# Splitting the context rows of a two-layer cross-attention kernel on ScalarE and VectorE instead of GpSimd, and the order in which two query groups are opened

## The chip, the cores and the metric

The kernel runs on one core of a Trainium2 chip. The metric is device time in microseconds (us), the median of several executions. A core has a matrix engine (TensorE, PE in the profile), a vector engine (VectorE, DVE), an activation engine (ScalarE, ACT), a general engine (GpSimd, POOL) and a queue engine that starts transfers (SyncE, SP). Each runs its own list of instructions in the order in which it was written; they meet at semaphores. PE writes to PSUM banks; ACT, DVE and POOL work on SBUF, and the first two also read PSUM.

## The reference

Two layers work on 2048 tokens of 256 features and on 1601 context rows of 256 features. Each layer is a cross attention followed by a mixture-of-experts network. The change lies in the cross attention of the second layer, where tokens attend to context and context to tokens:

```python
def _L1_xattn_ref(char_emb, subword_emb, ...):      # tokens, context
    ...
    scores = jnp.einsum('bqh,bkh->bqk', Q_char, K_sub) * scale
    char2sub = jnp.einsum('bqk,bkh->bqh', jax.nn.softmax(scores, axis=-1), V_sub)
    ...
    scores2 = jnp.einsum('bqh,bkh->bqk', Q_sub, K_char) * scale
    sub2char = jnp.einsum('bqk,bkh->bqh', jax.nn.softmax(scores2, axis=-1), V_char)
    L_char = char_emb.shape[1]
    if sub2char.shape[1] != L_char:
        sub2char = _interp_linear(sub2char, L_char)
    gate_in = jnp.concatenate([char2sub, sub2char], axis=-1)
    gate = jax.nn.sigmoid(jnp.einsum('blh,oh->blo', gate_in, Wg) + bg)
    return gate * char2sub + (1 - gate) * sub2char
```

`sub2char` has one row for each of the 1601 context rows; `_interp_linear` stretches it to 2048 rows, each a weighted mean of two neighbouring ones.

## The kernel before

**Precision.** TensorE multiplies numbers of a shortened float format. So each operand x is split in two: x_hi is x copied to that format, x_lo is x - x_hi. A product is then three matmuls: hi·hi, lo·hi, hi·lo (`mm3`, lines 43 to 45). Nearly every tile in the trace has the suffix `_hi` or `_lo` for that reason, and "a split" is a copy (often on ACT) and a subtraction (often on DVE).

**Groups, blocks, steps.** `cross_phase` does both attentions of the second layer. The queries stand in 14 groups. Groups 0 to 5 are the context rows (the "context half"): 13 row tiles of 128, two per group and three in group 5. Groups 6 to 13 are the 16 token tiles, two per group (a "token pair"). The keys of a group are cut in blocks, mostly two key tiles wide; all groups together have 112 blocks. Group 5 is blocks 40 to 55, group 6 blocks 56 to 62, group 7 blocks 63 to 69, group 8 blocks 70 to 76. The main part is a loop over steps n = 0 to 100, written out once for each engine; all its instructions have fixed places. For a block, in order of what depends on what:

- PE `score` (lines 43 to 45, output `wide`), ACT `evacuate` (line 2414) to a place in SBUF (tiles `Fx`, `sraw` or `X`), DVE `maximum` (line 2825 for the first block of a group, 2828 for the others; tile `rows`) and, at the last block of a group, a fold of the two halves (line 2832).
- Once per group: PE `max_turn` (line 2115, a transpose of the maxima), DVE `tops` (line 2838), ACT `spread_max` (line 2424), PE `spread_turn` (line 2122). After that the group's maximum lies on a PSUM bank, and the group can be opened.
- DVE `subtract` (line 2849), ACT `exponent` (line 2429), ACT `high` (line 2436, tile `pt`), DVE `low` (line 2854, tile `pt`), and PE `weighted` (lines 2140 to 2142), the product with the values. Step n holds `weighted(n)`; the others run ahead.
- After a group's last block DVE's `finish` (lines 2865 and 2879) divides by the sum, which frees PE's bank for the next group's first block. For a context tile the result is a row tile of `X`.

**What runs ahead by how much** is set by tables: `behind[n]` names the blocks whose scores stand in step n; `sub_end`, `exp_end` and `high_end` say up to which block the subtractions, the exponentials, and the high and low halves have come after step n. A group's subtractions start at step `open_from(g)`: 61 for group 7 and 68 for group 8. There `sub_end` jumps by four blocks, and `exp_end` follows a step later:

```python
sub_end = [reached(n, 5) for n in range(-1, NBLK)]
exp_end = [sub_end[0]] + sub_end[0:NBLK]
high_end = [min(reached(n, 2), e) for n, e in zip(range(-1, NBLK), exp_end)]
```

**Context rows.** The 13 finished row tiles in `X` are split into `CT_hi` and `CT_lo`, so that PE can interpolate them (`interpolate`, lines 2165 and 2166): a matmul with a "tent", a 128x128 matrix of interpolation weights. The first interpolation stands in step 61. The split is done in four pieces, `ROW_CHUNKS`: tiles 0-1, 2-5, 6-9 and 10-12. ACT copies the first two pieces to `CT_hi` (line 2562, steps 56 and 57); POOL copies the other two (line 2703) and subtracts all four (line 2707). All of it waits for the last block of the context half (`weighted_done` at `NSB` = 56). POOL makes the tents as well (`tents_of`: TENSOR_SCALAR in lines 2682 to 2689 and 2696, TENSOR_TENSOR in line 2690), four of them by the time of the first mixing; in its queue stand the tent of tile 0, the four row pieces, and the tents of tiles 1 to 3. The tents lie in the spare ends of `V_hi` and `V_lo`.

**Other work in these steps.** During group 5 PE also makes the keys and values of the token half (`later_unit`), whose high halves ACT copies (line 2392 for values) and whose low halves DVE subtracts (line 2811). At steps 47, 48, 49 and 57 one weight is split (`LATE`: lines 2591 and 3071).

## Time and profile before

| what | us |
|---|---|
| median of 3 runs | 978.98 |
| lowest and highest | 978.89, 980.35 |
| the profiled execution | 977.88 |
| its span, first to last instruction | 976.1 |
| PE busy in the span | 929.8 |
| DVE busy | 736.2 |
| ACT busy | 583.0 |
| POOL busy | 359.0 |

The span is what the profile shows of one execution; the few microseconds around it belong to starting and ending the program. PE's mean granted clock was 0.991 of full speed. A duration of a row is that of one execution of one instruction, or of several merged ones where it says x2 or more. Instructions on an engine overlap a little at their ends, so that a row of 0.68 us can be followed by the next start after 0.60 us.

### The profile page before, as it was taken

The page shows a single profiled execution, that of the slowest core. Times are in us where ns is not written, and L with a number is a line of the kernel's source. Part 1 is how long each engine was busy: PE and PEld are TensorE (multiplying, and loading weights), DVE is VectorE, ACT ScalarE, POOL GpSimd, SP SyncE. Part 2 cuts the span into 40 slices and gives each one's busy share as a digit, 9 for nine tenths or more (in the row PEclk, how much of TensorE's full clock was granted, in tenths as well). Part 3 has the DMA queues.
Part 4 walks back from the last instruction along what each step waited for, and adds up shares of the span by engine and source line. Part 5 has one row for each costly group of instructions (what it writes and reads, how often), then busy time and mean ns, then how long its engine had stood idle before and what let it go on. Part 6 is the DMA issues. An engine that isn't in the chain of part 4 may idle for free. (4 is left out here: it accounts for less than half of the span.)

```text
span 976.1 us, 19295 instructions
## 1 busy us (share of the span) xinstructions
PE 929.8 (95%) x6934; PEld 876.2 (90%) x6934; DVE 736.2 (75%) x1704; ACT 583.0 (60%) x1243; POOL 359.0 (37%) x512
## 2 busy tenths in 40 slices
PE   8999999899999999999899999999999799999996
PEld 8899998678899999998787899999899799999995
DVE  7677777668678888884576577767658868998987
ACT  6346666433377777774243577666557466667653
POOL 4514444516334444423561200000002945545552
PEclk9999999999999999999999999999999899999999
DMA  8200000021298788761421100000100000000100
GB/s 246 87 1 1 1 2 1 1 87 65 87 287 260 262 255 263 253 221 51 124 69 58 46 1 1 1 1 1 44 1 24 1 1 12 23 23 20 34 15 33
DMA packets 50947, 72.36 MB, mean 74 GB/s; under 512 B 5488, under 2 KB 33776, under 8 KB 50864
## 3 DMA queue, kind: packets, MB, share of 16 engines
q1 hardware_dynamic: 45152, 55.81, 18.3%
q0 software_dynamic: 5024, 14.42, 4.5%
q8 instruction: 49, 0.80, 0.3%
q10 hardware_dynamic: 688, 1.05, 0.3%
q14 instruction: 34, 0.28, 0.1%
HBM read 59.34 MB, written 11.93 MB: 73 GB/s over the span
## 5 line engine op out<-in xcount | busy, mean ns | idle before, releaser
L2140 PE MATMUL wide<-V_hi,pt 128*128 128x258 f32 x400 | 116.8, 292 | 3.2 <-DVE pt L2854 3.2
L2142 PE MATMUL wide<-V_hi,pt 128*128 128x258 f32 x400 | 113.9, 285 | 0.0
L2141 PE MATMUL wide<-V_lo,pt 128*128 128x256 f32 x400 | 113.4, 284 | 0.0
L2696 POOL TENSOR_SCALAR V_hi<-rows 128x256 fp32r<-128x256 f32 (+1 forms) x9 | 9.7, 1081 | 203.6 <-PE bank L2142 202.9
L2140 PEld LDWEIGHTS wide<-V_hi,pt 128*128 128x128 f32 x400 | 76.3, 191 | 3.8 <-DVE pt L2854 3.6
L2141 PEld LDWEIGHTS wide<-V_lo,pt 128*128 128x128 f32 x400 | 76.8, 192 | 0.2
L2142 PEld LDWEIGHTS wide<-V_hi,pt 128*128 128x128 f32 x400 | 76.5, 191 | 0.0
L43 PE MATMUL bank<-rx_hi,expert_w_hi 128*128 128x256 f32 x256 | 73.6, 288 | 1.6 <-PEq L1100 1.6
L45 PE MATMUL bank<-rx_hi,expert_w_lo 128*128 128x256 f32 x256 | 71.6, 280 | 0.0
L44 PE MATMUL bank<-rx_lo,expert_w_hi 128*128 128x256 f32 x256 | 71.5, 279 | 0.0
L503 POOL DMA_INDIRECT rxr<-token_rows,lists x39 | 56.9, 1458 | 27.6 <-issue 15.5
L43 PE MATMUL wide<-XT_hi,expert_w_hi 128*128 128x256 f32 (+1 forms) x216 | 63.9, 296 | 0.2 <-ACT Fx L2414 0.2
L45 PE MATMUL wide<-XT_hi,expert_w_lo 128*128 128x256 f32 (+1 forms) x216 | 62.5, 289 | 0.0
L44 PE MATMUL wide<-XT_lo,expert_w_hi 128*128 128x256 f32 (+1 forms) x216 | 62.4, 289 | 0.0
L2828 DVE TENSOR_TENSOR rows<-rows,Fx 128x512 f32<-128x512 f32 (+2 forms) x60 | 42.1, 702 | 24.5 <-ACT Fx L2414 23.6
L514 DVE TENSOR_TENSOR expert_w_lo<-sraw,expert_w_hi 128x1024 fp32r<-128x1024 f32 x39 | 47.4, 1223 | 15.8 <-ACT expert_w_hi L510 15.7
L1541 DVE TENSOR_TENSOR a0pt<-bank,a0pt 128x512 fp32r<-128x512 f32 x64 | 37.4, 584 | 27.9 <-ACT a0pt L1405 27.5
L1298 PE MATMUL bank<-a0pt,expert_w_hi 128*128 128x256 f32 x208 | 56.2, 301 | 1.4 <-issue 1.3
L43 PE MATMUL bank<-XT_hi,expert_w_hi 128*128 128x512 f32 x136 | 55.1, 405 | 1.5 <-PEq L1212 0.6
L43 PE MATMUL wide<-CT_hi,expert_w_hi 128*128 128x256 f32 (+1 forms) x192 | 55.2, 288 | 1.0 <-DVE XT_lo L2774 1.0
L45 PE MATMUL wide<-CT_hi,expert_w_lo 128*128 128x256 f32 (+1 forms) x192 | 54.9, 286 | 0.0
L44 PE MATMUL wide<-CT_lo,expert_w_hi 128*128 128x256 f32 (+1 forms) x192 | 54.9, 286 | 0.0
(540 smaller groups left out, 3617.6 us busy)
## 6 DMA issues: line engine op xcount, KB each, us to landing
sraw<-w1T SPq DMA_DIRECT2D x14, 512.0 KB, 4.7
sraw<-w3T SPq DMA_DIRECT2D x14, 512.0 KB, 5.1
sraw<-w2T SPq DMA_DIRECT2D x14, 512.0 KB, 5.1
raw_even<-w1T SPq DMA_DIRECT2D x11, 512.0 KB, 4.5
raw_even<-w3T SPq DMA_DIRECT2D x11, 512.0 KB, 4.9
raw_even<-w2T SPq DMA_DIRECT2D x11, 512.0 KB, 5.4
routed_results<-rys POOLq DMA_DIRECT2D x15, 256.0 KB, 4.5
X<-x SPq DMA_DIRECT2D x4, 512.0 KB, 6.3
```

Of the source, the lines that this page charges most:

```text
L43: pe.matmul(out, wh, xh, start=first, stop=False)
L44: pe.matmul(out, wh, xl, start=False, stop=False)
L45: return pe.matmul(out, wl, xh, start=False, stop=last)
L503: pool.indirect_dma_start(xr[:, j % 2, t, :], None, rows_in[:, :], bass.IndirectOffsetOnAxis(ap=lists[:, q:q + 1], axis=0))\
L514: dve.tensor_tensor(w_lo[:, par, piece(k)], raws[par][:, piece(k)], w_hi[:, par, piece(k)].bitcast(F32), ALU.subtract).then_inc(split_done ...
L1298: pe.matmul(ob[:, 0:2 * P], V_hi[:, k, :], both, start=k == 0, stop=False)
L1541: dve.tensor_tensor(weights(g, 1), transposed(g), weights(g, 0).bitcast(F32), ALU.subtract).then_inc(tlo, 1)
L2140: pe.matmul(dst[:, 0:D + 2], hi[:, x], v_hi(k), start=opens(n) and j == 0, stop=False)
L2141: pe.matmul(dst[:, 0:D], hi[:, x], v_lo(k), start=False, stop=False)
L2142: m = pe.matmul(dst[:, 0:D + 2], lo[:, x], v_hi(k), start=False, stop=closes(n) and k == keys_of(n)[-1])
L2696: pool.tensor_scalar(tent(i)[:, 0:n * P], d, 1.0, 0.0, ALU.add, ALU.max).then_inc(tent_done, 1)
L2828: dve.tensor_tensor(mx[:, 0:w], mx[:, 0:w], place(n), ALU.max).then_inc(maxed, 1)
```

## The change

Four things change.

1. `ROW_CHUNKS` has seven pieces of two row tiles (the last of one).
2. ACT copies each piece to `CT_hi`, and DVE, no longer POOL, subtracts it (`rows_to_low`). Piece k stands at the end of step `ROWS_AT[k]`: 45, 51, 52, 53, 57, 62, 63, on ACT and on DVE. The first four so lie in the context half. ACT waits only for the keys and values that still read the same columns, and for the finished rows.
3. POOL has no part in it; its tents of tiles 1 to 3 follow that of tile 0 at once.
4. At steps 61 and 68, where groups 7 and 8 are opened (`opening`), the subtraction of the group's first block comes first on DVE, and its exponential, high half and low half are done in the same step, a step earlier than before. Groups 9 to 13 are left as they were.

ACT's evacuation at step 61 of block 72, which overwrites the second row tile and later ones, now waits for ten split tiles instead of all 13, and block 76's waits for all 13.

```diff
@@ -1806,7 +1806,8 @@
                     m += 1
                 return m
             sub_end = [reached(n, 5) for n in range(-1, NBLK)]
-            exp_end = [sub_end[0]] + sub_end[0:NBLK]
+            opening = {open_from(g): first[g] + 1 for g in (SG + 1, SG + 2)}
+            exp_end = [sub_end[0]] + [max(sub_end[n], opening.get(n, 0)) for n in range(NBLK)]
             high_end = [min(reached(n, 2), e) for n, e in zip(range(-1, NBLK), exp_end)]
 
             with ExitStack() as ctx:
@@ -1872,7 +1873,8 @@
                     o = (NC + i % 4) * D
                     return X[:, o:o + D] if i % 4 < 3 else BV_C
 
-                ROW_CHUNKS = [(0, 2), (2, 6), (6, 10), (10, NC)]
+                ROW_CHUNKS = [(0, 2), (2, 4), (4, 6), (6, 8), (8, 10), (10, 12), (12, NC)]
+                ROWS_AT = [first[SG - 1] + k for k in (5, 11, 12, 13, 17)] + [NSB + 6, NSB + 7]
 
                 def rows_of(a, z):
                     return X[:, a * D:z * D].rearrange("p (r c n) -> p c r n", c=DC, n=P)
@@ -1941,8 +1943,8 @@
                  weighted_done, summed, reciprocals, finished) = sems(
                     ctx, "scored evacuated maxed folded max_turned topped spread spread_turned lowered exped high_done low_done "
                          "weighted_done summed reciprocals finished")
-                (row_known, tent_step, tent_done, rows_high, rows_copied, rows_split) = sems(
-                    ctx, "row_known tent_step tent_done rows_high rows_copied rows_split")
+                (row_known, tent_step, tent_done, rows_high, rows_split) = sems(
+                    ctx, "row_known tent_step tent_done rows_high rows_split")
                 (between, copied, mixed, turned, in_high, in_low, gated, biased, squashed, scaled, moved, stat, gathered, inv, normal,
                  x_turned, x_high, x_low, first_done, first_kept, soft_top, soft_less, soft, soft_exped, second_done, added, out_done,
                  stored) = sems(
@@ -2407,6 +2409,8 @@
                         if n < first[1]:
                             act.wait_ge(unit_low, 1 + max(UNITS.index(("v", k, 0)) for k in keys_of(n)))
                         if g == SG + 2 and n == first[g] + 2:
+                            act.wait_ge(rows_split, 10)
+                        if g == SG + 2 and n == first[g] + 6:
                             act.wait_ge(rows_split, NC)
                         if g == SG:
                             act.wait_ge(unit_low, 1 + max(UNIT_AT["t", 0] if k in EARLY else UNIT_AT["v", k] for k in keys_of(n)))
@@ -2555,16 +2559,12 @@
 
                     def rows_to_high(k):
                         a, z = ROW_CHUNKS[k]
-                        if k == 0:
-                            act.wait_ge(unit_done, END)
-                            act.wait_ge(weighted_done, NSB)
+                        act.wait_ge(unit_done, 1 + max(UNIT_AT["k", NKS - 1], UNIT_AT["t", 0], UNIT_AT["v", z - 1]))
                         act.wait_ge(finished, z)
                         act.activation(of_rows(CT_hi, a, z), rows_of(a, z), ACT.Copy).then_inc(rows_high, 1)
                     for n in range(END_AT):
                         b, u, v = post(n)
                         early_step(b, u, v)
-                        if NSB <= n < NSB + 2:
-                            rows_to_high(n - NSB)
                         for m in range(n, n + 6):
                             if exp_end[n] <= m < exp_end[n + 1]:
                                 exponent(m)
@@ -2581,6 +2581,8 @@
                         for g in range(1, NG):
                             if max_step(g) == n:
                                 spread_max(g)
+                        if n in ROWS_AT:
+                            rows_to_high(ROWS_AT.index(n))
                         if n in LATE:
                             k = LATE.index(n)
                             if k == 0:
@@ -2696,17 +2698,6 @@
                         pool.tensor_scalar(tent(i)[:, 0:n * P], d, 1.0, 0.0, ALU.add, ALU.max).then_inc(tent_done, 1)
                         pool.wait_ge(tent_done, i + 1)
 
-                    def split_rows(k):
-                        a, z = ROW_CHUNKS[k]
-                        if k >= 2:
-                            pool.wait_ge(finished, z)
-                            pool.tensor_copy(of_rows(CT_hi, a, z), rows_of(a, z)).then_inc(rows_copied, 1)
-                            pool.wait_ge(rows_copied, k - 1)
-                        else:
-                            pool.wait_ge(rows_high, k + 1)
-                        pool.tensor_tensor(of_rows(CT_lo, a, z), rows_of(a, z), of_rows(CT_hi, a, z).bitcast(F32),
-                                           ALU.subtract).then_inc(rows_split, z - a)
-
                     def mix(i):
                         pool.wait_ge(copied, i + 1)
                         pool.wait_ge(finished, NC + i + 1)
@@ -2729,8 +2720,6 @@
                     link(pool.tensor_copy(where, apart_m[:, 0:P].bitcast(I32)))
                     link(pool.tensor_scalar(where, where, 0.5 / S, None, ALU.mult))
                     tents_of(0)
-                    for k in range(len(ROW_CHUNKS)):
-                        split_rows(k)
                     for i in range(1, 4):
                         tents_of(i)
                     for i in range(11):
@@ -2993,6 +2982,12 @@
                     subtract(3)
                     subtract(4)
                     maximum(12)
+
+                    def rows_to_low(k):
+                        a, z = ROW_CHUNKS[k]
+                        dve.wait_ge(rows_high, k + 1)
+                        dve.tensor_tensor(of_rows(CT_lo, a, z), rows_of(a, z), of_rows(CT_hi, a, z).bitcast(F32),
+                                          ALU.subtract).then_inc(rows_split, z - a)
 
                     def soft_end(i):
                         for k in range(2, 8):
@@ -3051,9 +3046,11 @@
                         if closes(n):
                             for t in range(1, GROUPS[group_of[n]][1]):
                                 finish(group_of[n], t)
+                        if n in opening:
+                            subtract(sub_end[n])
                         for m in behind[n - 1] if n else ():
                             maximum(m)
-                        for m in range(sub_end[n], sub_end[n + 1]):
+                        for m in range(sub_end[n] + (n in opening), sub_end[n + 1]):
                             subtract(m)
                         for m in range(high_end[n], high_end[n + 1]):
                             low(m)
@@ -3065,6 +3062,8 @@
                         for g in range(1, NG):
                             if max_step(g) == n:
                                 tops(g)
+                        if n in ROWS_AT:
+                            rows_to_low(ROWS_AT.index(n))
                         if n in LATE:
                             hi, lo, src = late_weights[LATE.index(n)]
                             dve.wait_ge(late_high, LATE.index(n) + 1)
```

How the instructions stand now. On DVE, from `low(53)` in step 51 to `subtract(59)` in step 54, before; the TENSOR_REDUCE is the top reduction of group 6:

```order
L2854 TENSOR_TENSOR pt<-X,pt 128x322
L2811 TENSOR_TENSOR V_lo<-bank,V_hi 128x256
L2838 TENSOR_REDUCE top<-bank 128x2
L2854 TENSOR_TENSOR pt<-X,pt 128x322
L2811 TENSOR_TENSOR V_lo<-bank,V_hi 128x256
L2849 TENSOR_TENSOR Fx<-Fx,bank 128x512 x3
L2854 TENSOR_TENSOR pt<-X,pt 128x322
L2811 TENSOR_TENSOR V_lo<-bank,V_hi 128x256
L2849 TENSOR_TENSOR Fx<-Fx,bank 128x512
```

The same stretch in the changed kernel; line 2843 is `low`, 2838 is `subtract`, 2989 is `rows_to_low`:

```order
L2843 TENSOR_TENSOR pt<-X,pt 128x322
L2800 TENSOR_TENSOR V_lo<-bank,V_hi 128x256
L2827 TENSOR_REDUCE top<-bank 128x2
L2989 TENSOR_TENSOR CT_lo<-X,CT_hi 128x2x256
L2843 TENSOR_TENSOR pt<-X,pt 128x322
L2800 TENSOR_TENSOR V_lo<-bank,V_hi 128x256
L2989 TENSOR_TENSOR CT_lo<-X,CT_hi 128x2x256
L2838 TENSOR_TENSOR Fx<-Fx,bank 128x512 x3
L2843 TENSOR_TENSOR pt<-X,pt 128x322
L2800 TENSOR_TENSOR V_lo<-bank,V_hi 128x256
L2989 TENSOR_TENSOR CT_lo<-X,CT_hi 128x2x256
L2838 TENSOR_TENSOR Fx<-Fx,bank 128x512
```

Three subtractions of context rows stand behind the top reduction, the low half of block 54 and that of block 55.

On DVE at steps 60 (its end) and 61, and the start of step 62, before. The first row is `low(62)`, then `maximum(71)`, the subtractions of blocks 63 to 66, the two finishings of group 6, `maximum(72)`, `subtract(67)`, and `low(63)` with `low(64)`:

```order
L2854 TENSOR_TENSOR pt<-Fx,pt 128x256
L2828 TENSOR_TENSOR rows<-rows,Fx 128x512
L2849 TENSOR_TENSOR Fx<-Fx,bank 128x512 x4
L2865 RECIPROCAL inverse_sum<-wide 128x1
L2879 SCALAR_TENSOR_TENSOR sraw<-wide,inverse_sum,rows 128x256
L2865 RECIPROCAL inverse_sum<-wide 128x1
L2879 SCALAR_TENSOR_TENSOR sraw<-wide,inverse_sum,rows 128x256
L2828 TENSOR_TENSOR rows<-rows,X 128x512
L2849 TENSOR_TENSOR Fx<-Fx,bank 128x512
L2854 TENSOR_TENSOR pt<-Fx,pt 128x512 x2
```

The same stretch in the changed kernel:

```order
L2843 TENSOR_TENSOR pt<-Fx,pt 128x256
L2838 TENSOR_TENSOR Fx<-Fx,bank 128x512
L2817 TENSOR_TENSOR rows<-rows,Fx 128x512
L2838 TENSOR_TENSOR Fx<-Fx,bank 128x512 x3
L2843 TENSOR_TENSOR pt<-Fx,pt 128x512
L2854 RECIPROCAL inverse_sum<-wide 128x1
L2868 SCALAR_TENSOR_TENSOR sraw<-wide,inverse_sum,rows 128x256
L2854 RECIPROCAL inverse_sum<-wide 128x1
L2868 SCALAR_TENSOR_TENSOR sraw<-wide,inverse_sum,rows 128x256
L2817 TENSOR_TENSOR rows<-rows,X 128x512
L2838 TENSOR_TENSOR Fx<-Fx,bank 128x512
L2843 TENSOR_TENSOR pt<-Fx,pt 128x512
```

The first subtraction now stands ahead of `maximum(71)` (line 2817), and `low(63)` ahead of the finishings; a piece of the context rows stands behind `low(64)`.

On POOL, behind the tent of tile 0, before:

```order
L2696 TENSOR_SCALAR V_hi<-rows 128x128
L2707 TENSOR_TENSOR CT_lo<-X,CT_hi 128x2x256
L2707 TENSOR_TENSOR CT_lo<-X,CT_hi 128x2x512
L2703 CAST CT_hi<-X 128x2x512
L2707 TENSOR_TENSOR CT_lo<-X,CT_hi 128x2x512
L2703 CAST CT_hi<-X 128x2x384
L2707 TENSOR_TENSOR CT_lo<-X,CT_hi 128x2x384
L2686 TENSOR_SCALAR rows<-rows,row_f 128x128 x2
L2689 TENSOR_SCALAR rows<-rows 128x256
L2690 TENSOR_TENSOR rows<-rows 128x256
L2696 TENSOR_SCALAR V_hi<-rows 128x256
L2686 TENSOR_SCALAR rows<-rows,row_f 128x128 x2
```

In the changed kernel:

```order
L2698 TENSOR_SCALAR V_hi<-rows 128x128
L2688 TENSOR_SCALAR rows<-rows,row_f 128x128 x2
L2691 TENSOR_SCALAR rows<-rows 128x256
L2692 TENSOR_TENSOR rows<-rows 128x256
L2698 TENSOR_SCALAR V_hi<-rows 128x256
L2688 TENSOR_SCALAR rows<-rows,row_f 128x128 x2
L2691 TENSOR_SCALAR rows<-rows 128x256
```

The six instructions on context rows are gone, and the tents follow each other.

## Rows read from the trace of the kernel before

**Rows 1.** The page, section 1: busy us of engines (share of the span) xinstructions.

```profile
PE 929.8 (95%) x6934; PEld 876.2 (90%) x6934; DVE 736.2 (75%) x1704; ACT 583.0 (60%) x1243; POOL 359.0 (37%) x512
```

**Rows 2.** PE's waits, 745 to 810 us: us in total, times, longest.

```profile
PE bank L2115 <- DVE rows L2832: 3.8, 1, 3.8
PE wide L2140 <- DVE pt L2854: 3.2, 2, 1.8
```

**Rows 3.** PE's timeline: start, us, engine, line, operation, tiles [idle before <-releaser].

```profile
747.02 0.28 PE L2140 MATMUL wide<-V_hi,pt 128*128 128x258 f32 x1
...
760.40 0.28 PE L45 MATMUL wide<-XT_hi,expert_w_lo 128*128 128x256 f32 x1
...
764.52 0.69 PE L2115 MATMUL bank<-ident,rows 128*128 128x128 f32 x2 [3.84 <-DVE rows L2832]
764.86 0.57 PE L2140 MATMUL wide<-V_hi,pt 128*128 128x258 f32 x1
...
770.14 0.43 PE L2122 MATMUL bank<-ident,rows 128*128 128x128 f32 x2
...
777.65 0.39 PE L2140 MATMUL wide<-V_hi,pt 128*128 128x258 f32 x1 [1.84 <-DVE pt L2854]
...
806.04 0.39 PE L2140 MATMUL wide<-V_hi,pt 128*128 128x258 f32 x1 [1.34 <-DVE pt L2854]
```

**Rows 4.** Windows of PE: stretch, us, busy (instructions), granted clock, DMA share, GB/s.

```profile
765.00:766.00 1.00, 1.00 (x6) 0.50 0.00 0
776.00:778.00 2.00, 0.34 (x2) 1.00 0.00 0
```

**Rows 5.** DVE's timeline, 752 to 766 us.

```profile
752.42 2.55 DVE L2854 TENSOR_TENSOR pt<-Fx,pt 128x512 fp32r<-128x512 f32 x1 [0.44 <-ACT pt L2436]
754.89 1.52 DVE L3071 TENSOR_TENSOR expert_w_lo<-sraw,expert_w_hi 128x512 fp32r<-128x512 f32 x1
756.34 2.88 DVE L2828 TENSOR_TENSOR rows<-rows,Fx 128x512 f32<-128x512 f32 x1
...
760.38 2.29 DVE L2828 TENSOR_TENSOR rows<-rows,Fx 128x512 f32<-128x512 f32 x1
762.77 0.69 DVE L2828 TENSOR_TENSOR rows<-rows,X 128x512 f32<-128x512 f32 x1
...
764.04 0.43 DVE L2832 TENSOR_TENSOR rows<-rows 128x256 f32<-128x256 f32 x1
...
765.59 0.91 DVE L2825 COPY rows<-Fx 128x512 f32<-128x512 f32 x1
```

**Rows 6.** POOL's timeline, 752 to 766 us.

```profile
752.01 2.41 POOL L2707 TENSOR_TENSOR CT_lo<-X,CT_hi 128x1024 fp32r<-128x1024 f32 x1 [1.75 <-ACT CT_hi L2562]
...
762.11 1.97 POOL L2686 TENSOR_SCALAR rows<-rows,row_f 128x128 f32<-128x128 f32 x2
...
765.48 0.73 POOL L2690 TENSOR_TENSOR rows<-rows 128x256 f32<-128x256 f32 x1
```

**Rows 7.** DVE's timeline, end of the context half.

```profile
740.12 0.50 DVE L2854 TENSOR_TENSOR pt<-X,pt 128x322 fp32r<-128x322 f32 x1 [1.13 <-ACT pt L2436]
...
744.13 0.69 DVE L2854 TENSOR_TENSOR pt<-Fx,pt 128x512 fp32r<-128x512 f32 x1
745.10 0.17 DVE L2865 RECIPROCAL inverse_sum<-wide 128x1 f32<-128x1 f32 x1 [0.28 <-PE wide L2142]
745.30 0.48 DVE L2879 SCALAR_TENSOR_TENSOR X<-wide,inverse_sum,rows 128x256 f32<-128x256 f32 x1
```

**Rows 8.** ACT's timeline, end of the context half.

```profile
739.63 0.46 ACT L2436 ACTIVATE pt<-X 128x322 fp32r<-128x322 f32 x1
...
747.95 0.63 ACT L2562 ACTIVATE CT_hi<-X 128x512 fp32r<-128x512 f32 x1
```

**Rows 9.** DVE's timeline, opening of group 7.

```profile
772.01 2.47 DVE L2849 TENSOR_TENSOR Fx<-Fx,bank 128x512 f32<-128x512 f32 x4
...
776.92 1.82 DVE L2854 TENSOR_TENSOR pt<-Fx,pt 128x512 fp32r<-128x512 f32 x2
```

## Prediction

> **What bounds the kernel now.** I read four views in this order. First the busy line of the page: TensorE (PE) is busy for 929.8 of 976.1 us [rows 1], so only what shortens PE's work or closes its idle times can move the end. Second, PE's waits between 745 and 810 us [rows 2]: one wait of 3.8 us for line 2832, VectorE's (DVE's) last fold of a running maximum, and two, 3.2 us together, for line 2854, the low half of exponentiated scores. Third, PE's timeline [rows 3], which places them. Fourth, the timelines of DVE and GpSimd (POOL) at the long wait [rows 5, 6]: there DVE is not idle; its instructions are long.
>
> Gap A: PE starts a matmul at 760.40 and the next one, the transpose of the maximum, at 764.52 [rows 3]. It costs twice: 4.12 us, less about 0.12 that would pass anyway, is 4.0 us idle; then the granted clock is 0.50 (1.2 GHz) [rows 4], and the 24 matmuls from 764.86 to 770.14 take 5.28 us where the higher level (2.4 GHz) needs half, 2.6 us more. A is worth 4.0 + 2.6 = 6.6 us.
>
> Gap B, at 777.65: 1.84 us for the first low half of query group 7. Gap C, at 806.04: 1.34 us for that of group 8 [rows 3]. The first matmul behind each lasts 0.39 instead of 0.28 us, so I count 2.0 and 1.5 us. The clock stayed at 1.00 across B [rows 4]. Together the gaps hold 10.1 us.
>
> **Why A is there.** Four DVE instructions of 128x512 at 752.42, 754.89, 756.34 and 760.38 take 2.55, 1.52, 2.88 and 2.29 us; the same form takes 0.69 at 762.77 [rows 5]. The excess is 9.24 - 4 x 0.69 = 6.5 us. It lies beside POOL's splitting of context rows, whose subtractions last 2.41 us at 752.01, for instance [rows 6]; the DVE instruction of 752.42 ends at 754.97, about 0.5 us behind that one's end. The fold comes last in this queue and ends at 764.47 [rows 5].
>
> **Part 1: POOL no longer splits the rows.** This takes the 6.5 us off the DVE queue ahead of the fold. It also moves POOL's tents of tiles 1 to 3 forward, from 762 to about 747 us, beside the same DVE work. Their price: at 762.77 a DVE maximum runs in 0.69 us inside POOL's TENSOR_SCALAR pair of 762.11, so those cost nothing visible; POOL's TENSOR_TENSOR of 765.48 (0.73 us) meets a DVE copy that takes 0.91 us [rows 5, 6]. I take at most 0.73 us per tile, 0 to 2.2 us for three, and use 1.5.
>
> The Trainium skill (SBUF — State Buffer, Who interferes with whom) says that a DVE instruction with two SBUF inputs and a GpSimd one that reads SBUF block each other for the whole instruction. The long subtractions agree; the 0.69 us maximum inside a TENSOR_SCALAR does not. By the page every tent instruction would block; that is rival 3, priced from rows.
>
> **Part 2: seven splits on ScalarE (ACT) and DVE.** Each 128x512 half costs ACT 0.63 us (before, ACT did two, the first at 747.95) [rows 8] and DVE about 0.62, the spacing of four such subtractions at 772.01 [rows 9]; the last is half as wide. By place:
> - Step 45: one on each, where PE waits for nothing: 0.
> - Steps 51 to 53: three in a row, behind the top reduction of group 6. On DVE 3 x 0.62 = 1.9 us enter between that and the finishing of group 5. Queued behind are low(54) (740.12), three subtractions, low(55), low(56) (744.13) and the finishing [rows 7]. ACT's first copy enters just ahead of its 739.63 instruction [rows 8], for which DVE already waits 1.13 us, so that idle time does not absorb the load. low(56) ended at 744.82; 1.9 us later is 746.7, and PE needs it at 747.02 [rows 3]: covered. The first finish ended at 745.78 behind 0.28 us of idle time; 1.9 - 0.3 = 1.6 later is 747.4, and PE needs it at 747.02 too: **a new wait of 0.4 us**. Ends: 0 if DVE overlaps better; if each of the three also waits a whole ACT copy, 3 x (0.62 + 0.63) = 3.75 less 2.2 us of slack of low(56) is 1.5 us.
> - Step 57: one on each, ahead of the late weight: 0.6 us in the queue of the fold.
> - Steps 62 and 63: 0.62 and about 0.35 us behind low(64) and low(65). In the new order low(65) leaves two blocks of PE work to spare: 0.
>
> **The fold in the new queue.** 764.47 - 6.5 + 0.6 + 1.9 (carried from steps 51 to 53) + 1.5 (tents) = 762.0 if DVE never waits between. PE wants it at 760.5, or 760.9 with the 0.4 above. But DVE does wait: 0.44 us at 752.42 for an ACT instruction [rows 5], which comes earlier because ACT no longer has its 1024-column split ahead of it, and small excesses outside the four instructions go too. I expect the fold at 760 to 761.5 and take **0.3 us of wait**, with ends 0 and 2.2 (tents at full price, nothing absorbed). What is next late is low(61) and the top reduction behind it, both needed a block later. Without a long idle time the clock has no reason to drop as in A: it did not at B.
>
> **Part 3: the openings.** Now, when the spread maximum of group 7 is on PE's bank (turn at 770.14), DVE first does maximum(71), behind ACT's evacuation of it, then four subtractions (from 772.01, 2.47 us), two finishings and a maximum, and low(63) only at 776.92 [rows 9]. In the new order: subtract(63), maximum(71), three subtractions, low(63): six instructions of 0.62 = 3.7 us from the turn. The exponential and copy of ACT lie between the first and the last: 2 x 0.63 = 1.3 us beside 2.5 us of DVE work, covered. PE is ready 777.65 - 1.84 = 775.81, which is 5.5 us after the turn: margin 1.8 us. Next late is the finishing of group 6, which waits for PE's own block 62 and takes two times 0.6 us while PE scores for 1.4 us: just covered. B closes, 2.0 us. Group 8 has the same order, a smaller gap, and a turn that lies further ahead: C closes, 1.5 us. If finishing came out half a microsecond late each time, 1 us of the 3.5 would stay; the low end is that nothing is gained.
>
> **Sum.** 4.0 + 2.6 + 2.0 + 1.5 - 0.4 - 0.3 = 9.4 us. Behind 806 us PE has work waiting nearly all the time until 935, so what is gained there reaches the end. The profiled execution took 977.88 us (span 976.1), 1.1 below the median: 977.88 - 9.4 = 968.5 for it, and 978.98 - 9.4 = **969.6 us** for the median.
>
> **Rivals.**
> 1. DVE is still late at the fold, by 1 to 2.2 us: everything at its upper end. For it: 762.0 on paper. Against: waits of DVE absorb. With a low clock for part of a stretch it costs up to 3.5 us: 971.3 to 974. Chance 0.14.
> 2. The openings stay closed to PE by something else, the finishing of the group before: only A is gained, 6.6 - 0.7 = 5.9: 973. Against it stand the margins above. Chance 0.07.
> 3. POOL's tents block DVE in all their instructions. They fill POOL without a pause in the stretch before the fold, where 13 DVE instructions stand with two inputs in SBUF or as a copy. Against 6.5 us removed stand 0.6 + 1.9 = 2.5 of splits; at 0.3 us for each of the 13, 3.9 more, nothing is won at the fold, gap A stays, and the 3.5 us of the openings remain: 975.5. Chance 0.06. At 1 us each (one POOL instruction of the tents) the fold ends 13 + 2.5 - 6.5 = 9 us later than now, against a gain of 3.5: 984.5, slower than before. It tips to slower at (3.5 + 4.0) / 13, about 0.6 us each. The 0.69 us row speaks against it. Chance 0.02.
> 4. Less is changed than said, because the cause of A lies elsewhere, in ACT or PE's scores: within 2 us of 979. The new order of DVE's queue shows the splits and openings do move, and excess and POOL rows coincide. Chance 0.04.
>
> **How the numbers follow.** Forecast as derived, 968.3 to 971.3: 0.67. The range that should hold 8 in 10 takes rivals 1 and 2 in: 968.3 to 974.0; its low end is the 10.1 us with no new wait plus 0.6 for the spread of runs, its high end rival 1's. About 0.2% (2 us) is what a measurement of this kernel can tell from no change. Faster by more: 0.67 + 0.14 + 0.07 + most of rival 3's first case = 0.92. Within: 0.05. Slower: 0.03.
>
> **What would show it.** In the changed profile: the granted clock at 1.00 from 720 to 935; no row of POOL on context rows; DVE's 128x512 instructions between 749 and 763 at 0.7 us, some at 1.2; PE's waits on the fold under 0.5 us and on line 2843 (the old 2854) gone at both openings; a new small wait on the finishing of group 5 near 747. I am wrong if DVE instructions of 1.5 us and more stay beside the tents, if the wait near 747 is over 1.5 us, or if a turn or a first product takes the place of B and C.

## Result and profile after

The changed kernel takes 968.68 us (median of 4; 968.32 to 969.94), beside 978.93 for the kernel before (median of 4). The ratio is 0.9889, 95% interval 0.9877 to 0.9901, about 10.9 us less with 9.7 to 12.0 as its ends. The forecast was 9.4 us less (969.6). The ratio put on 978.98, the median that the prediction started from, gives 968.1, just under the low end of the stated range, 968.3.

The profiled execution took 969.94 us, the slowest of the four, with a span of 968.1. The page's busy line, as [rows 1]:

```profile
PE 929.1 (96%) x6934; PEld 876.1 (90%) x6934; DVE 731.4 (76%) x1711; ACT 584.9 (60%) x1248; POOL 352.6 (36%) x506
```

In these two profiles PE does the same work in 8 us less; the idle time of the gaps has gone, and so has the slow time behind gap A. PE's waits of 745 to 815 us, as [rows 2], are now one line, and its timeline at the places of [rows 3] has no wait mark:

```profile
PE bank L43 <- DVE XT_lo L2873: 0.3, 1, 0.3
```

```profile
746.52 0.39 PE L2142 MATMUL wide<-V_hi,pt 128*128 128x258 f32 x1
...
749.34 0.36 PE L2142 MATMUL wide<-V_hi,pt 128*128 128x258 f32 x1
...
762.91 0.38 PE L2117 MATMUL bank<-ident,rows 128*128 128x128 f32 x2
...
771.46 0.29 PE L2142 MATMUL wide<-V_hi,pt 128*128 128x258 f32 x1
...
798.26 0.28 PE L2142 MATMUL wide<-V_hi,pt 128*128 128x258 f32 x1
```

The transpose of group 7's maximum (762.91, line 2117, before 2115) follows the last score matmul at once. The first products of groups 7 and 8 (771.46 and 798.26, line 2142, before 2140) last 0.29 and 0.28 us, like any other, where they were 0.39 after a wait. The clock, as [rows 4] (stretch, us, busy, granted clock, DMA share, GB/s):

```profile
580.00:585.00 5.00, 5.00 (x30) 0.66 0.01 3
715.00:720.00 5.00, 4.93 (x43) 1.00 0.00 0
765.00:770.00 5.00, 5.00 (x44) 1.00 0.00 0
```

The granted clock is 1.00 in the stretch of gap A. The fall at 580 has nothing to do with the change; the last section comes back to it. DVE, where [rows 5, 7] stood (line 2989 is the new subtraction of context rows, 2843 `low`, 2817 `maximum`, 2868 a finishing, 2821 the fold):

```profile
746.72 0.68 DVE L2989 TENSOR_TENSOR CT_lo<-X,CT_hi 128x512 fp32r<-128x512 f32 x1
...
747.91 0.68 DVE L2843 TENSOR_TENSOR pt<-Fx,pt 128x512 fp32r<-128x512 f32 x1
...
748.71 0.48 DVE L2868 SCALAR_TENSOR_TENSOR X<-wide,inverse_sum,rows 128x256 f32<-128x256 f32 x1
...
754.56 0.90 DVE L2843 TENSOR_TENSOR pt<-Fx,pt 128x512 fp32r<-128x512 f32 x1
756.76 0.69 DVE L2989 TENSOR_TENSOR CT_lo<-X,CT_hi 128x512 fp32r<-128x512 f32 x1 [1.30 <-ACT CT_hi L2564]
...
757.97 0.78 DVE L2817 TENSOR_TENSOR rows<-rows,Fx 128x512 f32<-128x512 f32 x1
758.67 0.92 DVE L2843 TENSOR_TENSOR pt<-Fx,pt 128x512 fp32r<-128x512 f32 x1
759.51 0.68 DVE L2817 TENSOR_TENSOR rows<-rows,Fx 128x512 f32<-128x512 f32 x1
760.44 0.89 DVE L2817 TENSOR_TENSOR rows<-rows,X 128x512 f32<-128x512 f32 x1 [0.25 <-ACT X L2418]
...
761.90 0.43 DVE L2821 TENSOR_TENSOR rows<-rows 128x256 f32<-128x256 f32 x1
```

and POOL, as [rows 6], with the tents of tiles 1 and 2 (lines 2688 to 2698):

```profile
751.38 2.07 POOL L2691 TENSOR_SCALAR rows<-rows 128x256 f32<-128x256 f32 x1
753.53 1.38 POOL L2692 TENSOR_TENSOR rows<-rows 128x256 f32<-128x256 f32 x1
...
758.64 1.08 POOL L2691 TENSOR_SCALAR rows<-rows 128x256 f32<-128x256 f32 x1
759.80 0.98 POOL L2692 TENSOR_TENSOR rows<-rows 128x256 f32<-128x256 f32 x1
```

No DVE instruction here is over 0.92 us. Sometimes it is POOL that stretches: the TENSOR_SCALAR of 751.38 takes 2.07 us beside DVE instructions that stay at 0.68 us, and the same one at 758.64 takes 1.08 us beside a DVE instruction of 0.92. The fold ends at 762.33, half a microsecond ahead of PE.

The prediction put the long DVE rows of [rows 5] beside POOL's splitting as a whole. POOL's rows of before tell its two kinds apart:

```profile
754.36 1.50 POOL L2703 CAST CT_hi<-X 128x1024 fp32r<-128x1024 f32 x1
756.01 2.66 POOL L2707 TENSOR_TENSOR CT_lo<-X,CT_hi 128x1024 fp32r<-128x1024 f32 x1
```

DVE's 2.55, 2.88 and 2.29 us stand beside subtractions of 2.41, 2.66 and 2.06 us, and each DVE instruction ends 0.55 us behind its POOL instruction. But the 1.52 us of 754.89 stand beside this CAST, which reads one tile only: one-input instructions of POOL were not all free.

### The profile page after: what moved, and what is told of

Read it like the earlier page. It is cut to its first block and busy times, and to the rows that moved or that the text cites. A ratio compares the mean times of both kernels' runs of the same rounds, so it can differ in the third digit from the quotient of the medians.

```text
span 968.1 us, 19310 instructions
## 1 busy us (share of the span) xinstructions
PE 929.1 (96%) x6934; PEld 876.1 (90%) x6934; DVE 731.4 (76%) x1711; ACT 584.9 (60%) x1248; POOL 352.6 (36%) x506
## 3 DMA queue, kind: packets, MB, share of 16 engines
q10 hardware_dynamic: 688, 1.05, 0.3%
## 5 line engine op out<-in xcount | busy, mean ns | idle before, releaser
L44 PE MATMUL bank<-XT_lo,expert_w_hi 128*128 128x512 f32 x136 | 53.9, 397 | 0.0
```

What stands on the lines that cost most here:

```text
L44: pe.matmul(out, wh, xl, start=False, stop=False)
```

## The experiments

**How they were read.** Executions of one kernel differ by up to 5 us here (16 of the kernel before: 977.8 to 982.9), so the parts are read from one profile of each kernel by two distances on TensorE: T1, from group 5's transpose of the maximum (three 128x128 matmuls) to group 6's, and T2, from group 6's to group 9's. T2 holds the gaps A, B and C, and the pieces from step 51 on; T1 holds the pieces of steps 44 to 48. Behind T2 nothing differs: from group 9's transpose to TensorE's last matmul it is 151.9 us both before and after.

| kernel | start, group 5 | group 6 | group 9 | T1 | T2 | sum |
|---|---|---|---|---|---|---|
| before | 685.23 | 737.98 | 817.26 | 52.75 | 79.28 | 132.03 |
| changed | 688.96 | 739.87 | 809.39 | 50.91 | 69.52 | 120.43 |
| changed, again | 691.08 | 741.99 | 811.50 | 50.91 | 69.51 | 120.42 |
| order of the openings alone | 687.87 | 740.66 | 816.10 | 52.79 | 75.44 | 128.23 |
| rows alone | 686.34 | 738.83 | 812.13 | 52.49 | 73.30 | 125.79 |
| new order for all groups | 685.96 | 738.46 | 807.98 | 52.50 | 69.52 | 122.02 |
| all pieces late | 685.66 | 738.39 | 810.50 | 52.73 | 72.11 | 124.84 |
| POOL, needless TENSOR_TENSOR | 689.53 | 740.45 | 810.76 | 50.92 | 70.31 | 121.23 |
| POOL, needless TENSOR_SCALAR | 689.09 | 740.03 | 810.42 | 50.94 | 70.39 | 121.33 |
| POOL splits, early | 691.02 | 743.67 | 812.66 | 52.65 | 68.99 | 121.64 |
| pieces sooner | 685.72 | 739.75 | 808.79 | 54.03 | 69.04 | 123.07 |
| POOL splits, short instructions | 689.31 | 742.10 | 817.78 | 52.79 | 75.68 | 128.47 |
| idle time put in | 688.44 | 739.36 | 815.50 | 50.92 | 76.14 | 127.06 |
| pieces two and two | 689.58 | 741.46 | 810.70 | 51.88 | 69.24 | 121.12 |

The changed kernel's two profiles, 3.4 us apart in total, agree within 0.01 us in both distances: 2.1 us of the 3.4 lie ahead of group 5, 1.3 behind TensorE's last matmul. T1 comes in two sorts, about 1.6 us apart: with a granted clock of 0.66 over 715 to 720 us (or just behind it) in some executions, and at 1.00 in others. The changed kernel's two profiles are of the sort without, that with the new order for all groups (the same code up to there) is of the sort with, as is that of before. So 122.02 is to be compared with the 132.03 of before: **10.0 us for the change.**

**The two parts.** The order of the openings alone, in the kernel before:

```diff
+            opening = {open_from(g): first[g] + 1 for g in (SG + 1, SG + 2)}
-            exp_end = [sub_end[0]] + sub_end[0:NBLK]
+            exp_end = [sub_end[0]] + [max(sub_end[n], opening.get(n, 0)) for n in range(NBLK)]
...
+                        if n in opening:
+                            subtract(sub_end[n])
...
-                        for m in range(sub_end[n], sub_end[n + 1]):
+                        for m in range(sub_end[n] + (n in opening), sub_end[n + 1]):
```

> The kernel before with part 3 alone: the first subtraction of groups 7 and 8 first in steps 61 and 68, POOL still splits the context rows. Theory (two separate causes): gap A of 3.8 us and the low clock behind it stay, the waits of 1.8 and 1.3 us for the first low half go; 3.5 us less than before, 975.5. Rival (the openings were late only because A and POOL's splitting had made DVE late, or finishing comes next): they stay; 978 to 979.

977.01 us (9 executions; ratio 0.9971, 0.9954 to 0.9987), and PE's waits of 745 to 815 us:

```profile
PE bank L2116 <- DVE rows L2833: 3.8, 1, 3.8
PE bank L43 <- DVE XT_lo L2885: 0.3, 1, 0.3
```

The long wait is whole, both waits on a low half are gone: 3.8 us less by the distances. The openings were late by their own order. The rows alone, in the changed kernel:

```diff
-            opening = {open_from(g): first[g] + 1 for g in (SG + 1, SG + 2)}
+            opening = {}
```

> The changed kernel without part 3: rows split on ACT and DVE, openings in the order of before. Theory: A goes with its low clock, 6.6 us less (972.3), both opening waits stay at 1.3 to 1.9 us. Rival (openings late only because of A's delay): all 10 us gained by this part alone, 969.

974.50 us (8 executions; ratio 0.9956, 0.9934 to 0.9979):

```profile
PE wide L2142 <- DVE pt L2843: 3.2, 2, 1.9
PE bank L43 <- DVE XT_lo L2873: 0.3, 1, 0.3
```

The mirror image: 6.2 us less, A gone, both openings waiting as before. 132.03 - 125.79 = 6.24 and 132.03 - 128.23 = 3.80 add up to 10.04: the parts are independent. The medians of these runs show 2.8 and 4.3 us, 1 to 2 us too little, within their spread. The changed kernel again:

> The changed kernel once more, beside its parts. Theory: 968 to 969.5, with two opening waits and gap A gone; if 1 us or more of its distance to the sum of the parts (10.1 us) comes from elsewhere, its trace shows it ahead of 700 us.

969.70 us (6 executions, 967.23 to 973.30; ratio 0.9896, 0.9878 to 0.9915). And the new order for groups 9 to 12 too:

```diff
-            opening = {open_from(g): first[g] + 1 for g in (SG + 1, SG + 2)}
+            opening = {open_from(g): first[g] + 1 for g in range(SG + 1, NG - 1)}
```

> The changed kernel with the new opening order also for groups 9 to 12. Theory: PE waits for no first low half of these groups, so nothing is gained: within 0.5 us of the changed kernel's 968.7. Rival (the order itself costs DVE or ACT, each of which stands still for the other at an opening): 0.5 to 2 us slower than that, with new waits of PE on a low half or on a finishing.

970.65 us (6 executions, 968.38 to 974.00). Its T2 is the changed kernel's, and behind group 9's transpose, where the new order works, TensorE takes the same 151.9 us to its last matmul. Nothing is gained or lost: where PE does not wait, the order is free.

**Is it the place?** All seven pieces behind the context half:

```diff
-                ROWS_AT = [first[SG - 1] + k for k in (5, 11, 12, 13, 17)] + [NSB + 6, NSB + 7]
+                ROWS_AT = [NSB + k for k in (0, 1, 2, 3, 4, 6, 7)]
```

> The changed kernel with all seven pieces of the context rows behind the context half, at steps 56, 57, 58, 59, 60, 62, 63, on ACT and DVE. From group 6's transpose of the maximum to group 9's TensorE takes 79.3 us in the kernel before and 69.5 in the changed one. Theory (place matters as well as engine): in the queue of group 7's fold stand 3 more pieces of 0.6 us between 748 and 760 in place of the 3 at steps 51 to 53, which carried over 1.9 us; since those are then absent, the fold is late by the difference, 0 to 1 us, and each piece makes DVE wait for ACT: 70 to 71.5 us for the stretch. Rival (only POOL's part mattered, place is free): 69.0 to 69.6.

971.99 us (4 executions; ratio 0.9930, 0.9902 to 0.9958), T2 72.11, more than expected:

```profile
PE bank L2117 <- DVE rows L2821: 1.6, 1, 1.6
PE wide L2142 <- DVE sraw L2868: 1.1, 1, 1.1
```

A wait on the fold comes back at 1.6 us, and one on the finishing of group 6 (line 2868) at 1.1. DVE, 759 to 766 us:

```profile
759.43 0.81 DVE L2989 TENSOR_TENSOR CT_lo<-X,CT_hi 128x512 fp32r<-128x512 f32 x1 [2.03 <-ACT CT_hi L2564]
...
765.12 0.69 DVE L2989 TENSOR_TENSOR CT_lo<-X,CT_hi 128x512 fp32r<-128x512 f32 x1 [1.35 <-ACT CT_hi L2564]
```

The pieces cost DVE 0.6 us each and, more, its idle time for ACT's copy: 1.24 and 2.03 us ahead of group 7's fold, 1.35 and 0.97 us between the fold and the finishing of group 6. By the sums, all of the same sort and with the openings in their new order: 128.23 with the split on POOL, 124.84 with all pieces late, 122.02 as changed. Taking the work off POOL brings 3.4 of the rows' 6.2 us even in this place, the place the other 2.8.

Sooner instead:

```diff
-                ROWS_AT = [first[SG - 1] + k for k in (5, 11, 12, 13, 17)] + [NSB + 6, NSB + 7]
+                ROWS_AT = [first[SG - 1] + k for k in (4, 5, 6, 8, 17)] + [NSB + 6, NSB + 7]
```

> The changed kernel with its first four pieces at steps 44, 45, 46 and 48 in place of 45, 51, 52 and 53. Measured from group 5's spread maximum on TensorE (the three transposes of 128x128) to group 9's transpose of the maximum. Theory (the 0.4 us that TensorE loses at 744 to 747 comes from three pieces carried on DVE behind group 6's top reduction): that wait goes and nothing else changes, 0.4 us less. Rival (the pieces collide with value tiles and the late weights at steps 47 to 49): a wait of 0.5 to 1.5 us at group 6's fold or at evacuations near 727 to 740.

971.21 us (5 executions; ratio 0.9906, 0.9890 to 0.9921). T2 falls by 0.5 as expected, but T1 rises by 1.5 (54.03 beside 52.50), in sum 1.05 more: the rival holds. In 685 to 745 us:

```profile
PE wide L43 <- ACT Fx L2418: 1.4, 1, 1.4
```

ACT's evacuation waits for the bias column that DVE makes beside the value tile, and in DVE's queue this stands behind the piece of step 48 and a late weight. Two and two (steps 45, 46, 51, 52) was the last try:

```diff
-                ROWS_AT = [first[SG - 1] + k for k in (5, 11, 12, 13, 17)] + [NSB + 6, NSB + 7]
+                ROWS_AT = [first[SG - 1] + k for k in (5, 6, 11, 12, 17)] + [NSB + 6, NSB + 7]
```

> The changed kernel with its first four pieces at steps 45, 46, 51 and 52 in place of 45, 51, 52 and 53: one piece less behind group 6's top reduction, none at the crowded steps 47 to 49. Theory: TensorE's 0.4 us at 744 to 747 go, and no wait comes at the evacuations near 735, since DVE still has over 1 us of idle time at steps 46 and 47: from group 6's to group 9's transpose of the maximum 69.0 to 69.2 us, and 52.5 (with a low clock near 715) or 50.9 (without) from group 5's to group 6's. The total is then 0.3 to 0.5 us less than the changed kernel's, too little for a comparison of medians. Rival (any piece before step 50 delays the value tiles and with them an evacuation): a wait of TensorE of 0.3 us or more near 735.

969.82 us (6 executions; ratio 0.9895, 0.9877 to 0.9913), T2 0.3 less, T1 1.0 more (51.88 beside 50.91, the same sort), in sum 0.7 more, with the same wait at 0.9 us. The rival holds again. None of the places tried beats the changed kernel's.

**Is it POOL, and which of its instructions?** Twelve needless instructions, four behind each of tents 1 to 3, results unused:

```diff
+                        if 1 <= i < 4:
+                            for _ in range(4):
+                                link(pool.tensor_tensor(m, d, m, ALU.add))
```

> The changed kernel with 12 needless TENSOR_TENSOR of 128x256 on POOL, four behind each of the tents 1 to 3 (some 9 us of POOL work, result unused). Theory (a POOL instruction with two SBUF inputs holds up DVE for its whole length): DVE's 128x512 instructions between 750 and 785 lengthen by 0.3 to 0.7 us each where they meet one, 4 to 8 us together, and a wait at a fold, a finishing or a low half comes back: stretch 71 to 75 us against 69.5. Rival (gap A came from the order in DVE's queue, POOL was a bystander): no DVE row over 1.0 us, 69.5 us.

> As the run with needless TENSOR_TENSOR, but with 12 needless TENSOR_SCALAR of 128x256 (one SBUF input, some 13 us of POOL work). Theory (POOL's TENSOR_SCALAR gives way: it lengthens itself, from 1.07 to 2 us in the changed kernel, DVE hardly): DVE excess under 2 us in all and a stretch of 69.5 to 70.5 us. Rival (every POOL instruction that reads SBUF blocks a DVE one with two inputs): more excess than with TENSOR_TENSOR, since the time is longer, 73 us and up.

The second has `pool.tensor_scalar(m, d, 0.0, -2.0, ALU.max, ALU.mult)` in the same place. Both kernels were run once. T2 is 70.31 and 70.39 us, 0.8 and 0.9 more. POOL and DVE with the TENSOR_TENSORs:

```profile
757.05 4.18 POOL L2702 TENSOR_TENSOR rows<-rows 128x256 f32<-128x256 f32 x4
```

```profile
757.34 1.00 DVE L2992 TENSOR_TENSOR CT_lo<-X,CT_hi 128x512 fp32r<-128x512 f32 x1 [1.31 <-ACT CT_hi L2564]
758.27 1.23 DVE L3073 TENSOR_TENSOR expert_w_lo<-sraw,expert_w_hi 128x512 fp32r<-128x512 f32 x1
759.41 1.23 DVE L2820 TENSOR_TENSOR rows<-rows,Fx 128x512 f32<-128x512 f32 x1
760.56 1.22 DVE L2846 TENSOR_TENSOR pt<-Fx,pt 128x512 fp32r<-128x512 f32 x1
```

and with the TENSOR_SCALARs:

```profile
756.65 5.59 POOL L2702 TENSOR_SCALAR rows<-rows 128x256 f32<-128x256 f32 x4
```

```profile
757.55 0.68 DVE L3073 TENSOR_TENSOR expert_w_lo<-sraw,expert_w_hi 128x512 fp32r<-128x512 f32 x1
758.15 0.88 DVE L2820 TENSOR_TENSOR rows<-rows,Fx 128x512 f32<-128x512 f32 x1
758.96 0.68 DVE L2846 TENSOR_TENSOR pt<-Fx,pt 128x512 fp32r<-128x512 f32 x1
759.56 0.88 DVE L2820 TENSOR_TENSOR rows<-rows,Fx 128x512 f32<-128x512 f32 x1
```

Beside the two-input POOL instructions four DVE instructions in a row take 1.00 to 1.23 us, 2.0 us over 0.68 each. Beside the one-input ones the four DVE rows shown take 0.68 to 0.88, 0.4 us over, while POOL's own take 1.4 us each on average instead of 1.08. For DVE both theories hold. For the end the first was overrated: with the TENSOR_TENSORs PE waits only 0.57 us for the fold, and T2 stays under the 71 that was expected. With the TENSOR_SCALARs the time returned elsewhere, as a wait of 0.67 us on a spread maximum (line 2124) at 792.

Short instructions in the kernel before, one row tile each:

```diff
-                            pool.tensor_copy(of_rows(CT_hi, a, z), rows_of(a, z)).then_inc(rows_copied, 1)
...
+                            for r in range(a, z):
+                                m = pool.tensor_copy(of_rows(CT_hi, r, r + 1), rows_of(r, r + 1))
...
+                        for r in range(a, z):
+                            pool.tensor_tensor(of_rows(CT_lo, r, r + 1), rows_of(r, r + 1), of_rows(CT_hi, r, r + 1).bitcast(F32),
+                                               ALU.subtract).then_inc(rows_split, 1)
```

> The kernel before with POOL's copies and subtractions of context rows cut to one row tile each (128x256), same place and same work otherwise. Theory (a long POOL instruction with two SBUF inputs holds DVE up for its whole length; with short ones DVE gets in between): DVE's 128x512 instructions take 1.0 to 1.3 us instead of 1.5 to 2.9, gap A shrinks from 3.8 us to 0 to 2 us and the clock stays up, 3 to 6 us less than before (973 to 976). Rival (what counts is POOL's total time beside DVE): gap A 3.5 us or more, since the total rises with more instructions; 979 or more.

977.07 us (5 executions; ratio 0.9953, 0.9936 to 0.9970), T2 75.68, 3.6 less than before. DVE:

```profile
759.13 1.23 DVE L2831 TENSOR_TENSOR rows<-rows,Fx 128x512 f32<-128x512 f32 x1
760.28 0.88 DVE L2857 TENSOR_TENSOR pt<-Fx,pt 128x512 fp32r<-128x512 f32 x1
...
762.17 0.94 DVE L2831 TENSOR_TENSOR rows<-rows,X 128x512 f32<-128x512 f32 x1 [0.21 <-ACT X L2414]
```

```profile
PE wide L2140 <- DVE pt L2857: 3.7, 2, 2.4
PE bank L2122 <- ACT rows L2424: 0.5, 1, 0.5
```

The same split on the same engine in the same place, and DVE's 2.88 us of [rows 5] are at most 1.23; gap A is gone. POOL takes longer for it, 16.8 us instead of 11.4, and gap B grows from 1.84 to 2.40. So of A it was not POOL's total time but the length of its single instructions that counted.

T2 understates this, for it holds a low clock far from gap A. Behind gap C, here 1.33 us, the granted clock falls:

```profile
805.87 0.42 PE L2142 MATMUL wide<-V_hi,pt 128*128 128x258 f32 x1
```

The clock is at 0.50 from about 805.4 to 808.8, where matmuls like this one take 0.42 instead of 0.28 us. Laid beside the same matmuls of the kernel with the rows alone, this costs 1.5 us. Without it T2 would be 74.1, 5.1 less than before. Gap C of before, 1.34 us, had no such fall.

Early instead of short: POOL does all seven pieces, five of them in the context half, ACT and DVE none:

```diff
-                        if n in ROWS_AT:
-                            rows_to_high(ROWS_AT.index(n))
...
+                    def split_rows(k):
+                        a, z = ROW_CHUNKS[k]
...
+                        pool.wait_ge(finished, z)
+                        pool.tensor_copy(of_rows(CT_hi, a, z), rows_of(a, z)).then_inc(rows_high, 1)
+                        pool.wait_ge(rows_high, k + 1)
+                        pool.tensor_tensor(of_rows(CT_lo, a, z), rows_of(a, z), of_rows(CT_hi, a, z).bitcast(F32),
+                                           ALU.subtract).then_inc(rows_split, z - a)
...
+                    for k in range(5):
+                        split_rows(k)
                     tents_of(0)
+                    split_rows(5)
+                    split_rows(6)
...
-                        if n in ROWS_AT:
-                            rows_to_low(ROWS_AT.index(n))
```

> The changed kernel with POOL doing copy and subtraction of all seven pieces, the first five as soon as the value tiles that read the same columns are done (about 712 to 735 us), the last two behind the context half; ACT and DVE have none. Theory (the time at which POOL works matters, not that it is POOL): in the context half DVE has slack of 1 to 2 us a block, so the first five are hidden, and the last two cost DVE about 2 us near 750 where their own 3 x 0.6 no longer stand: stretch 69.5 to 70.5 us. Rival (POOL beside DVE always costs): the excess shows at group 6's fold (a wait of 0.5 us now) or at low halves, 2 to 5 us.

971.16 us (4 executions; ratio 0.9907, 0.9883 to 0.9932). T2 is 68.99, the lowest of all; but T1 is 52.65, and its clock is of the sort without the low stretch, so 1.7 us more than the changed kernel's 50.91:

```profile
PE wide L43 <- ACT Fx L2418: 1.1, 1, 1.1
```

Theory and rival each hold for a part: in T2 POOL costs nothing, in T1, where its first five pieces run beside DVE, 1.7 us, most in one evacuation near 740. In sum 1.2 us more than the changed kernel.

**What the idle time costs.** The changed kernel, in which PE's transpose of group 7's maximum also waits for the fourth tent:

```diff
                     def max_turn(g):
                         pe.wait_ge(folded, g + 1)
+                        if g == SG + 1:
+                            pe.wait_ge(tent_done, 4)
```

> The changed kernel in which TensorE's transpose of group 7's maximum also waits for the fourth tent of POOL (at about 767.7 us in the changed profile, 4.8 us behind the place where TensorE wants to go on). Nothing else is late. Theory (the idle time itself brings the clock of 1.2 GHz, as in gap A): the stretch from group 6's to group 9's transpose grows from 69.5 us by 4.8 plus 2 to 3 us of low clock, 76.5 to 77.5. Rival (the low clock behind A had another cause): 74.3, clock 1.00.

Run once, 976.04 us:

```profile
767.08 0.66 PE L2119 MATMUL bank<-ident,rows 128*128 128x128 f32 x2 [4.52 <-issue]
```

```profile
764.00:766.00 2.00, 0.00 (x0) 0.65 0.00 0
766.00:768.00 2.00, 0.92 (x5) 0.50 0.00 0
...
770.00:772.00 2.00, 2.00 (x13) 0.65 0.00 0
772.00:774.00 2.00, 2.00 (x19) 1.00 0.00 0
```

T2 grows by 6.6 us for 4.5 us of wait, so 2.1 us are low clock, and 76.14 is just under the expected 76.5. The profile names no releaser for this wait ("issue"). The clock fell during the idle time and is back at 1.00 from 772, while in both profiles of the changed kernel, without the wait, it does not fall here: the idle time itself brings it.

## Why the prediction was right, and where it was off

- **Gap A, worth 4.0 + 2.6, and its cause.** Right. Rows alone gives 6.2 net where the prediction's terms give 6.6 - 0.7 = 5.9. From group 6's transpose to group 7's it is 3.5 us less (26.54 before, 23.04 after), which is the 4.0 less 0.5 of new waits; from group 7's to group 8's 2.5 us less with the rows alone (28.14, 25.64), which is the low clock, put at 2.6. DVE's rows fell to 0.68 to 0.92 us, and short POOL instructions alone took the wait away. The low clock was checked by itself: 2.1 us for 4.5 us of wait. Of the 6.5 us of excess 0.8 lay beside a CAST, the rest beside subtractions.
- **The tents beside DVE, 1.5 us of 0 to 2.2.** Right in kind; in the changed kernel the excess of the DVE rows shown between 754 and 761 us is about 0.2 + 0.1 + 0.2 + 0.2 = 0.7 us. The prediction had twice as much.
- **The new wait of 0.4 us at steps 55 and 56.** Right in place and nearly in size. PE's start at 746.52 comes 0.1 us late, that at 749.34 0.23 us (348 ns behind the matmul ahead of it instead of 118), each with a matmul some 0.1 us longer: 0.5 us. DVE's first finish ends at 749.19, as reckoned behind low(56) (747.91). What was missed is a gain: PE's 0.19 us wait on an evacuation, at 734.67 before, is gone, and T1 is 0.25 us shorter at equal clock. With all pieces late the wait is there again (T1 52.73), so the gain goes with the pieces in the context half; why a piece there removes the wait stays open.
- **The wait of 0.3 us at the fold.** Wrong, 0: the tents were overrated and the queue's end, 762.0 on paper, was at 760.4 on the clock of before (762.33 less the 1.9 us by which this profile is late at group 6's transpose), where PE wants the fold at 761.0.
- **The openings, 2.0 + 1.5.** Right, mis-sized by 0.3: 2.2 + 1.6.
- **Rivals.** 1 (still late at the fold) fell; it is what happens if the pieces stand behind the context half. 2 (something else holds the openings) fell: alone they give their full worth. 3 (tents block as the splits did) fell: beside POOL's TENSOR_SCALARs DVE instructions grew by 0.1 us each, not 0.3. 4 (A has another cause) fell.
- **The step that failed** is the low end of the range, with two terms of the sum behind it. The terms gave 9.4; the distances have 10.0. The wait of 0.3 at the fold was 0, the gain of 0.25 in T1 was put at nothing, and the openings gave 0.3 more; the new wait was 0.1 more and the low clock 0.1 less. Even so, 10.0 us less is 969.0, inside the range. What took the result out of it is the allowance for the spread of runs: below the 10.1 us of the gaps (968.9) the range left 0.6 us, with three executions, 1.5 us apart, to go by. Sixteen executions of the kernel before range over 5 us, and the interval of the ratio alone is 1.2 us on either side. The comparison came out at 10.9, 0.9 more than the profiles give to the change, and 968.1 lies 0.2 under the stated end. That it fell there and not inside is luck: the second comparison of the changed kernel (0.9896) gives 968.8. A low end of 967.7, 1.2 below 968.9, would have covered the first as well.

The Trainium skill (SBUF — State Buffer, Who interferes with whom) has a DVE instruction with two SBUF inputs and a GpSimd one that reads SBUF block each other fully, by issue order. The 2.2 us delays of before, the 0.3 to 0.55 us beside 128x256 TENSOR_TENSORs, and POOL's own stretching to 2.07 us agree, and so do the 0.8 us beside a one-input CAST; that DVE lost only about 0.1 us beside each TENSOR_SCALAR is less than the rule's whole length.

## To carry to other kernels

When a DVE instruction takes two to four times its usual time, look at what POOL runs at that moment: here a two-input DVE instruction beside a POOL subtraction of 2.1 to 2.7 us lasted about as long as that one, so move such work, or cut it in pieces of one tile. Count the idle time of the matrix engine with the low clock behind it, here 2.1 to 2.5 us for 4 to 4.5 us of idle; gaps of 1.3 to 2.4 us had no low clock behind them, but for one of 1.33 us that cost 1.5. And place added work on DVE by who stands behind it in the queue: the same pieces cost 0.2 us net where the change has them, 0.7 more with one of them moved to step 46, 1.1 more with three at steps 44, 46 and 48, and 2.8 more behind the context half.

## What the runs showed of the hardware

Executions of one kernel on one chip spread over 5 us, and granted clock and time go together, if not strictly: the changed kernel's second set took 967.23 to 970.44 us at 0.993 to 0.996 and 972.21 to 973.30 at 0.990 to 0.991. Part of this are spells of 3 to 4 us at 0.50 (0.66 over a window of five microseconds, about 1.6 us lost) at places where PE is busy without a wait: at 580 to 585 in the profile after, not in that of before, and at 715 to 720 the reverse. In that of before, and what stands ahead of it:

```profile
712.85 0.27 PE L43 MATMUL bank<-expert_w_hi,CT_hi 128*128 128x2 f32 x1
...
714.77 0.25 PE L45 MATMUL bank<-expert_w_hi,CT_lo 128*128 128x2 f32 x1
```

```profile
715.00:720.00 5.00, 5.00 (x31) 0.66 0.00 0
```

These are the first and the last of 18 matmuls in a row with two columns each, about 2 us of them, and the clock falls at 715.6. Ahead of the fall at 581 in the profile after, 18 matmuls of the same 128x2 form stand at 578.0 to 580.1. All 14 profiles have one of these two falls, none has both, and none falls behind a third such row (516 to 518 in that of before). So by the busy share alone PE looks fully at work where its columns are few. That these narrow matmuls bring the fall is argued from their place; no run takes them away. Why the one row is followed by the fall in some executions and the other in the rest stays open. The spells are no part of the change: each profile holds one of the two, but T1 sees only the one at 715.
